# Second attention of a two-layer block: rows turned once and spread by transfers, sums of squares and scalings cut in two, the output's two parts added on leaving PSUM, a projection over 256 rows

## What is computed

```
def _L1_attn_ref(x, w_qkv, q_norm_w, k_norm_w, w_proj, b_proj):
    H = 16; D = dim // H                        # 16 heads of 16 features
    qkv = jnp.einsum('bld,ed->ble', x, w_qkv)
    q, k, v = (qkv[0], qkv[1], qkv[2])          # each (batch, head, token, 16)
    q = rmsnorm(q, q_norm_w)
    k = rmsnorm(k, k_norm_w)
    scores = jnp.einsum('bhqd,bhkd->bhqk', q, k) * D ** (-0.5)
    attn = jax.nn.softmax(scores, axis=-1)
    out = jnp.einsum('bhqk,bhkd->bhqd', attn, v)
    out = out.transpose(0, 2, 1, 3).reshape(B, L, dim)
    return jnp.einsum('bld,ed->ble', out, w_proj) + b_proj
```

## Time and profile before

| | |
|---|---|
| median of 3 runs | 1409.03 us (1408.11 to 1411.0) |
| profiled execution | 1408.91 us |
| its span, first to last instruction | 1407.1 us |
| busy in the span: PE, DVE, ACT, POOL | 97%, 65%, 58%, 54% |
| second layer, from its first transpose to the end | 890.0 to 1407.1 us |
| of it the slots with scores | 918.7 to 1386.2 us |

### The profile page before, as it was taken

The page is one execution under the profiler, slowest core; times in us unless marked ns, Lnnn a source line. Parts: engine busy times, 40 slices in busy tenths (PEclk is TensorE's granted clock), DMA queues, the critical chain, the costliest instruction groups (busy, mean ns, idle before and its releaser), DMA issues. The chain is left out here.

```text
span 1407.1 us, 25856 instructions
## 1 busy us (share of the span) xinstructions
PE 1368.9 (97%) x8950; PEld 1221.1 (87%) x8950; DVE 920.9 (65%) x1793; ACT 820.0 (58%) x2172; POOL 761.9 (54%) x757
## 2 busy tenths in 40 slices
PE   9999899999999999999999999899999999999997
PEld 7887798999899989998999888788889888889887
DVE  6655566565656565656665665677777878777764
ACT  5553444554544555445544544378787788778873
POOL 2651433454434454435544443477669677777764
PEclk9999999999999999999999999999999999999999
DMA  5995333334332343223433334144233242342442
GB/s 197 323 330 198 85 91 89 92 80 120 100 94 52 101 130 99 75 75 98 114 86 94 113 75 165 68 122 150 83 98 123 68 150 84 120 120 92 143 122 90
DMA packets 85681, 165.64 MB, mean 118 GB/s; under 512 B 16720, under 2 KB 27664, under 8 KB 83248
## 3 DMA queue, kind: packets, MB, share of 16 engines
q1 hardware_dynamic: 85552, 163.99, 38.3%
HBM read 99.90 MB, written 22.09 MB: 87 GB/s over the span
## 5 line engine op out<-in xcount | busy, mean ns | idle before, releaser
L775 POOL TENSOR_TENSOR a_pr<-a_pr,a_ri 128x512 f32<-128x512 f32 x128 | 133.5, 1043 | 299.1 <-DVE a_ri L955 299.1
L832 ACT ACTIVATE a_pr<-a_score,a_nb 128x256 f32<-128x256 f32 x256 | 119.3, 471 | 266.3 <-DVE a_nb L947 266.3
L1337 POOL TENSOR_TENSOR l_pr<-l_pr,l_ri 128x512 f32<-128x512 f32 x128 | 133.5, 1043 | 119.0 <-DVE l_ri L1714 118.1
L1465 ACT ACTIVATE l_pr<-l_score,l_nb 128x256 f32<-128x256 f32 x256 | 119.2, 472 | 80.8 <-DVE l_nb L1680 80.2
L58 PE MATMUL a_job<-s_xs,s_wh 128*128 128x512 f32 x384 | 153.9, 401 | 1.0 <-PEq L221 1.0
L60 PE MATMUL a_job<-s_xs,s_wl 128*128 128x512 f32 x384 | 151.7, 395 | 0.0
L59 PE MATMUL a_job<-s_xs,s_wh 128*128 128x512 f32 x384 | 151.3, 394 | 0.0
L947 DVE TENSOR_REDUCE a_nb<-a_score 128x2 f32<-128x512 f32 x128 | 88.5, 692 | 85.0 <-PE a_score L1026 83.3
L1680 DVE TENSOR_REDUCE l_nb<-l_score 128x2 f32<-128x512 f32 x128 | 87.5, 684 | 34.0 <-PE l_score L1820 33.4
L960 DVE TENSOR_TENSOR a_pt<-a_turn,a_pt 128x512 fp32r<-128x512 f32 x128 | 87.5, 683 | 24.2 <-ACT a_pt L840 24.2
L1844 PE MATMUL l_out<-s_wh,l_vp 128*128 128x256 f32 x512 | 91.6, 300 | 0.9 <-DVE s_wh L1684 0.9
(11 more groups left out here) (257 smaller groups left out, 4780.3 us busy)
## 6 DMA issues: line engine op xcount, KB each, us to landing
s_wl<-wgu_scratch SPq DMA_DIRECT2D x56, 512.0 KB, 4.8
a_sk<-a_rotk SPq DMA_DIRECT2D x384, 64.0 KB, 2.0
a_sq<-a_rotq SPq DMA_DIRECT2D x256, 64.0 KB, 2.0
s_xs<-xn_scratch SPq DMA_DIRECT2D x14, 1024.0 KB, 5.6
l_wd<-wd_scratch SPq DMA_DIRECT2D x56, 256.0 KB, 2.7
a_raw<-in_w SPq DMA_DIRECT2D x30, 256.0 KB, 3.0
wgu_scratch<-f_split SPq DMA_DIRECT2D x14, 512.0 KB, 4.7
f_praw<-in_moe_w SPq DMA_DIRECT2D x14, 384.0 KB, 4.5
```

The source lines that it names most:

```text
L775: pool.tensor_tensor(e, e, ri[:, n % 2, :].unsqueeze(2).broadcast_to([P, 2, SEQ]), ALU.mult)\
L832: i = act.activation(pr[:, n % 2, t, :], PS[n % 2][:, t * SEQ:(t + 1) * SEQ], ACT.Exp, bias=nb[:, n % 2, t:t + 1], accum_out=sm[:, n % 2, ...
L1337: pool.tensor_tensor(e, e, ri[:, n % 3, :].unsqueeze(2).broadcast_to([P, 2, SEQ]), ALU.mult)\
L1465: i = act.activation(pr[:, n % 3, t, :], PS[n % NPS][:, t * SEQ:(t + 1) * SEQ], ACT.Exp, bias=nb[:, n % 3, t:t + 1], accum_out=sm[:, n % 3 ...
```

## The change

- The jobs `S0` to `S7` of a sequence are replaced by `X0`, `X1` in slots 9 and 10: four transposes each, of 128 columns of q and of k in float32, with the heads' columns in another order in the weights (`head_columns`). ACT copies the result to `tqk` as the high part, DVE subtracts for the low part. SP stores `tqk` to DRAM (four transfers for each job), and loads it again, two pairs of heads at a time, spread and doubled as `zq` and `sk` need it (five transfers for each load, 32 loads). `zq` and `sk` have four places instead of three. TensorE waits for these loads at every fourth scores.
- `k_hi`, `q_hi`, `k_lo`, `q_lo` are gone. The copy to `qk` moves from DVE to ACT.
- Sums of squares and scaling are done for q in one slot and for k in the next (2 and 3, 7 and 8). The features of a head lie 4 (q) or 8 (k) elements apart, and the sum reads them in that distance. The Newton steps and the weights start one slot later; the weights are those of q alone, as before.
- The values' low parts now fill columns that lie 64 apart from the high parts. ACT copies the 64 rows of one part to the other half of the partitions (`out_low`), DVE adds them to the other 64 rows (`out_sum`), and two groups of four heads share a tile of 128 rows. ACT and DVE split that tile (`out_hi`, `out_lo`, now from SBUF, once for eight heads). The projection is over 2 blocks of rows, 6 matmuls for each job, and its weights are one piece of 512 columns.
- The planner's numbers: a projection job 6 units for 12, 28.1 units for a slot instead of 30.6, 18 instead of 14 in the slots ahead of the first scores.

```diff
-    NJ, NPS, NSTK, NGU, ND, NCB, NHID = 3, 1, 3, 3, 3, 3, 3
+    NJ, NPS, NSTK, NGU, ND, NCB, NHID = 3, 1, 4, 3, 3, 3, 3
+    PER_LOAD = 2
-    UNIT, SLOT_GOAL, EARLY_GOAL = 10, 30.6, 14
+    UNIT, SLOT_GOAL, EARLY_GOAL = 10, 28.1, 18
+    def X_AT(m):
+        return (9, 10)
-        m, r = divmod(n + 4, H1)
-        if r % 2 == 0 and 0 <= m < BATCH:
-            jobs.append((f"S{r // 2}", m))
+        if b + 1 < BATCH and u in X_AT(b + 1):
+            jobs.append((f"X{X_AT(b + 1).index(u)}", b + 1))
...
+                def store_stack(m, half):
+                    wait_free(sp, (f"X{half}", m))
+                    for low in range(2):
+                        sp.dma_start(qs_dram[m % 2, half, :, :, low].rearrange("h d p n -> (h d) p n"), tqk[:, half, 0, low, :].bitcast(F32))                           .then_inc(tqk_out[half], 16)
+                        sp.dma_start(ks_dram[m % 2, half, :, low].rearrange("h d p n -> (d p) h n"), tqk[:, half, 1, low, :].bitcast(F32))                           .then_inc(tqk_out[half], 16)
+                def load_stack(i):
+                    pair = i * PER_LOAD
+                    m, p = divmod(pair, H1 // 2)
+                    at = slice(pair % NSTK, pair % NSTK + PER_LOAD)
+                    if p % 4 == 0:
+                        sp.wait_ge(tqk_out[p // 4], 16 * 4 * (m + 1))
+                    if pair >= NSTK:
+                        sp.wait_ge(S["score_full"], 2 * (pair + PER_LOAD - NSTK))
+                    half, j = divmod(p, 4)
+                    for h in range(2):
+                        own = qs_dram[m % 2, half, h, :, :, j:j + PER_LOAD].rearrange("d c p n -> (d c) (p n)")
+                        for base in (64 * h, 64 * h + 32):
+                            sp.dma_start(zq[base:base + 32, h, at, :].bitcast(F32).rearrange("k p n -> k (p n)"), own)                               .then_inc(zq_in[stack_of(i)], 16)
+                    own = ks_dram[m % 2, half, :, :, :, j:j + PER_LOAD].rearrange("h c d p n -> (h c d) (p n)")
+                    sp.dma_start(sk[:, at, :].bitcast(F32).rearrange("r p n -> r (p n)"),
+                                  own.unsqueeze(1).broadcast_to([4 * D1, 2, PER_LOAD * SEQ])).then_inc(sk_in[stack_of(i)], 16)
+                def transfers(n):
+                    m, u = n // H1 + 1, n % H1
+                    if m < BATCH and u - 1 in X_AT(m):
+                        store_stack(m, X_AT(m).index(u - 1))
+                    if n % (2 * PER_LOAD) == 0 and 0 <= n // (2 * PER_LOAD) + 1 < N // (2 * PER_LOAD):
+                        load_stack(n // (2 * PER_LOAD) + 1)
...
                     if 2 <= K < L:
+                        stack_until(AT["U", K - NGU] if K >= NGU else SLOTS[0])
                         load_gu(K)
                     if K >= 1:
+                        stack_until(AT["D1", K - 1 - ND] if K > ND else SLOTS[0])
                         load_d(K - 1)
...
-                        act.activation(sqr[:, int(name[1]), :], bank[:, :], ACT.Square).then_inc(S["sq_ready"], 1)
+                        act.activation(sqr[:, :, int(name[1]), :], bank[:, :].rearrange("p (r n) -> p r n", r=2), ACT.Square).then_inc(S["sq_ready"], 1)
+                        if m >= 1 and name == "Q0":
+                            wait_full(act, ("X1", m - 1))
+                        act.activation(qk[:, :, int(name[1]), :], bank[:, :].rearrange("p (r n) -> p r n", r=2), ACT.Copy)\
+                           .then_inc(free_of(item), 1)
...
+                def out_low(g):
+                    here, there = VHALF * (g % 2), VHALF * (1 - g % 2)
+                    act.wait_ge(S["pv_done"], 4 * g + 4)
+                    act.activation(ol[here:here + VHALF, :], PO[there:there + VHALF, 0:SEQ], ACT.Copy).then_inc(S["out_low"], 1)
...
+                    elif name[0] == "X":
+                        half = int(name[1])
+                        dve.wait_ge(S["turned_hi"], 2 * m + half + 1)
+                        dve.tensor_tensor(tqk[:, half, :, 1, :], bank[:, :].rearrange("p (r n) -> p r n", r=2),
+                                          tqk[:, half, :, 0, :], ALU.subtract).then_inc(free_of(item), 1)
...
+                def sum_squares(m, r):
+                    q = (4, 8)[r]
...
+                    own(dve.tensor_reduce(by_head(ss, r, q), sqr[:, r].rearrange("p t (g d q) -> p (t g) q d", d=D1, q=q), AX.X, ALU.add))
...
+                def out_sum(g):
+                    here = VHALF * (g % 2)
+                    dve.wait_ge(S["out_low"], g + 1)
+                    if g >= 4:
+                        dve.wait_ge(S["out_lo"], (g - 4) // 2 + 1)
+                    dve.tensor_tensor(os[here:here + VHALF, g // 2 % VB, :], PO[here:here + VHALF, 0:SEQ], ol[here:here + VHALF, :], ALU.add)\
+                       .then_inc(S["out_free"], 1)
...
-                    if u % 2 == 0:
-                        wait_free(pe, (f"S{u // 2}", m))
+                    if u % (2 * PER_LOAD) == 0:
+                        i = n // (2 * PER_LOAD)
+                        pe.wait_ge(zq_in[stack_of(i)], 16 * 4 * (n // (2 * NSTK) + 1))
+                        pe.wait_ge(sk_in[stack_of(i)], 16 * (n // (2 * NSTK) + 1))
```

218 lines of the change are left out of this document (100 added, 118 removed).

## The result

The changed kernel takes 1414.12 us, the median of six runs (1412.8 to 1415.69), against 1410.01 us of the kernel before beside it (1408.11 to 1411.16): a ratio of 1.003, 95% interval 1.002 to 1.0041. The forecast was 1385 with a range of 1370 to 1402, so the change is slower by 0.3% where faster was forecast. The profiled execution took 1415.69 us, 30.1 more than the sum of 1385.6.

What follows compares the result with a forecast made beforehand. The prediction took TensorE to bound the stretch between first and last scores: 1408.9 - 16.8 (turning jobs) - 11.0 (projection) + 3.5 (first operands) + 1.0 (the end) = 1385.6, stated as 1385 us, range 1370 to 1402.

Steps and rivals of the forecast that it cites:

- TensorE's work: Second layer's TensorE stream: fewer turning jobs save 16.8 us, halved projection 11.0; 5.6 us of feed-forward pieces move ahead of the slots.
- First operands: Before the first scores: TensorE newly waits for zq and sk loaded from DRAM, +3.5 us.
- a wait of 2.2 us: Before the first scores: the wait if the 256 KB load lands in the skill's 2.6 us, not the measured row's 3.9.
- The end: After the last values: two ScalarE and VectorE steps become four, so the last projection begins later, +1.0 us.
- Later loads: The other 31 loads of zq and sk: one late by 0.6 us in sequence 4; 0 taken for all.
- the rival of late loads: Loads in the slots: 256 KB landing after 8 us makes 19 loads late, 34 us, total 1420; chance 0.06.
- VectorE's instructions: VectorE in the slots: removed and added instructions net -13.5 us, at the other end -8; share 0.78 against 0.756.
- the rival's assumption: VectorE's sums of squares: reading every fourth or eighth element doubles them to 1.2 us, 9.7 us more on VectorE.
- Waits in the slots: TensorE's waits between first and last scores: change taken as 0, bounds -12 and +15 us.
- VectorE as the bound: Slots: VectorE becomes the bound, 6 to 20 us over the forecast, 1392 to 1406, middle 1399; chance 0.22.
- Slots that stay as long as they were: Slots: waiting replaces the removed work slot by slot, slots stay at 3.66 us, total 1409; chance 0.03.
- the circle of scores, maximum and exponentials: Each slot: these steps run in a circle over one bank, said to add up to some 2.5 us.

## Why the prediction was wrong

**TensorE's work: right.** Jobs of X take 0.35 us (968.77 to 969.12), the projection is half, and of 32.0 us less between the first and the last scores some 31 came.

**First operands: right, but not the start.** The wait was 4.57 for a forecast of 3.5 within 2.7 to 5. Not seen was the wait of 3.12 at X0, behind the scalings, at the start, and the half clock behind both waits: the start cost 4.4 more than forecast. The section of the Trainium skill that the prediction names for a wait of 2.2 us (DMA: Bandwidth & Descriptors, "Anatomy of one DMA") is about transfers that GpSimd issues. Here SP issues them, and the wait of 4.57 does not bear that price out.

**The end: right by luck.** Its +1.0 was forecast for the longer way to the last projection, and +1.0 was measured for the whole stretch, which also holds 1.4 us saved in that projection. The longer way cost twice its price: the last projection starts 17.8 us behind the last scores, where it started 15.8 behind them. The last split on VectorE took 1.48 us instead of 0.41, beside an addition of GpSimd's; the others took 0.40 (median):

```profile
1405.30 1.64 POOL L1394 TENSOR_TENSOR l_y<-l_y,l_s 128x512 f32<-128x512 f32 x1 [5.99 <-DVE l_y L1700]
1405.74 1.48 DVE L1687 TENSOR_TENSOR l_ot<-l_os,l_ot 128x256 fp32r<-128x256 f32 x1
```

**Later loads: right, in part by luck.** One load of 31 came late, by 0.56; forecast were 0.6 for one. It was another one (load 24; the tight one in sequence 4 came 0.14 us ahead of its use). So the rival of late loads did not happen, though transfers took longer than the row they were priced by (below). The slots with preparation stayed 3.65 us long instead of 3.4, and so gave the loads more cover than forecast.

**VectorE's instructions: right but for two.** In the slots, the sums of the output took 417 ns and the splits 406, at the lower of two prices, X's subtraction 691. The sums at a distance took 1110, which was the rival's assumption (1.2 us) and not the forecast's, and scalings 1144 instead of 679, since they now stand beside GpSimd's gates, probabilities and weights.

**The step that failed: "Waits in the slots", taken as 0 with bounds of -12 and +15; it was about +22.** It was worked out from VectorE's share over 150 us of slots, as if waits followed from an average. The share did not even rise (0.755 for a forecast of 0.78), and the waits rose by some 22. What sets the time is the longest engine of the single slot, where one fills it: in slot 3 VectorE, in slots 8 and 9 mostly GpSimd or VectorE. Before, the longest engine beside TensorE was 0.2 to 0.8 us shorter than its slot on the mean, and as long in single ones (GpSimd 3.92 of 3.92 in slot 9 of sequence 4). So "TensorE bounds" was true, but with a small margin in the slots with preparation, and the change lengthened the peaks besides (VectorE in slot 3 from 2.72 to 3.90). The runs show both parts: without the longer peaks 5.3 (sums) and 7.1 (weights) come back, and 8.6 together with the later projection; with TensorE's work put back into those slots, 1.6 of 8.3 us show. These peaks are about a third of the 24.8 us that are missing in these slots; 2.8 more lie in the slot behind the end of a step, and no run took the rest apart.

**The rivals.** VectorE as the bound was the nearest in kind, for its cause (the doubled sums) and its sign of what is waited for. Its price of 1392 to 1406 was too low because it too was made from shares. Slots that stay as long as they were, given 0.03, describes the slots with preparation (-2.4 of -27.2), but not by its reason: the circle of scores, maximum and exponentials allows 3.25 us, as the last 19 slots show.

## What to carry over

Where several engines work through a chain in order, slot by slot, price a saving by the longest engine of each kind of slot, not by shares over the whole: subtract it in one slot and look at who is as long there already. Of an edit that moves an instruction, look at what will stand beside it on the engines that work on the same memory. Work that is taken off the bounding engine counts in full only where nothing else is prepared.
